# Second half of an attention kernel: half-width weights for Yh, relative outputs in 64 x 64 tiles of the array that fill two banks in turn, eight PSUM banks, eight residual tiles

## The chip, the cores and the metric

The kernel runs on one core of a Trainium2 chip. The metric is the time of one execution on the device in microseconds (us). Its engines are TensorE (PE: matmuls; PEld: their weight loads), VectorE (DVE), ScalarE (ACT), GpSimd (POOL) and SyncE (SP, which issues DMAs here). Matmuls write to PSUM, eight banks of 128 partitions x 512 floats.

## The reference

Eight images, 256 channels, 64 x 64 pixels, 8 heads of 64 channels. `Ix` picks from the table of relative positions.

```python
qkv = einsum('bcxy,oc->boxy', group_norm(x), w_qkv); q, k, v = split(qkv, 3)
k = softmax(k, axis=-1)
context = einsum('ndm,nem->nde', k, v)
content_out = einsum('nde,ndm->nem', context, q)
Px = einsum('xir,rd->xid', Ix, rel_rows);    Sx = einsum('ndxy,xid->nixy', q4, Px)
Yh = einsum('nixy,neiy->nexy', Sx, v4)
Yh = batch_norm(Yh)                          # mean and variance over images, heads and pixels
Py = einsum('yir,rd->yid', Iy, rel_columns); Sy = einsum('ndxy,yid->nixy', q4, Py)
rel_pos_out = einsum('nixy,nexi->nexy', Sy, Yh)
out = einsum('bcxy,oc->boxy', content_out + rel_pos_out, w_out) + b_out
return x + out
```

## The kernel before

The batch norm of Yh needs all images, so the kernel has two halves. The first (to about 1980 us) computes q, the context and Yh and stores them in DRAM. The second, which the change is about, goes over the images again. Every float32 operand is split into a high and a low float16 part, and a product is three matmuls (`TERMS`: high x high, high x low of the second, low of the first x high).

Heads are handled in pairs: `hp` is 0 to 3, head `h` of a pair lies on partitions 64h to 64h+63, and t = 4 x image + hp. The work is cut in tiles that each fill one PSUM bank, of three kinds:

- `sy` (L942), eight a head pair: Sy from q and the table of columns. 32 matmuls of 64 columns; each has 64 weight columns and writes 64 partitions, so a tile uses half the array's columns.
- `ro` (L956 and L962), eight a head pair: the output of 8 of the 64 rows x. The content part (L956) is 8 matmuls of 256 columns. The relative part (L962) is, for each x, three matmuls with 128 x 128 weights from `yb_hi` or `yb_lo` and 64 columns of `sy_hi` or `sy_lo`. These weights are block diagonal: `yb_hi[:, a, h, e, x]` holds head h's Yh on its own 64 partitions, and zeros on the other 64, which POOL writes once (L1141 to L1143).
- `pr` (L976), sixteen an image: the projection, 12 matmuls of 512 columns, for 128 channels and 512 pixels.

`turn2_of` writes the order of the tiles out for the first, a middle and the last image. `sy` tiles of the next head pair stand between the `ro` tiles of this one (`SY_BEFORE`), and the projection of an image between the `ro` tiles of hp 3 and of hp 0 of the next image. All engines go through this order. Tile number n uses bank n mod `BANKS` (5); before it PE waits until DVE has freed that bank (`freed`), so it can be five tiles ahead. ACT takes the high part out of the bank (L1028, L1033), DVE the low part (L1110, L1118), which frees it. For `pr`, ACT adds the bias to a tile of x (`x_res`, four of them, L1023) and DVE adds the bank to it (L1134); this waits for the tile's load from DRAM.

Between the tiles, after each odd `ro`, ACT (L996) and DVE (L1096) split a quarter of the normalised Yh of the next head pair, in two instructions of 64 partitions each, one per head, since the two go to different columns of `yb`. POOL normalises Yh (L1153, L1156). SP loads q for the head pair after next in four chunks, each as soon as a pair of `ro` tiles no longer needs the old one (L851, waits for `filled`), then Yh of the pair after that (L857, 2 MB), the context (L863) and the tiles of x (L869), all in one queue. PE waits for q at the first `sy` tile of a head pair.

Of the kernel before, what the change touches and what calls it, by code (L numbers as in the profile page):

```python
# [29 lines left out]
P = 128  # L30
GN_EPS = 1e-5
BN_EPS = 1e-5
TINY = 1e-30
BANKS = 5
BANK = 512
YST = 2
# [6 lines left out]
def attention_kernel(nc, x, w_qkv_t, w_out_t, b_out, rel_rows_t, rel_cols_t, gamma, beta,  # L43
# [59 lines left out]
    with ExitStack() as top:  # L103
# [8 lines left out]

        bank = ps("bank", [P, BANKS, BANK])
        ctx_ps = ps("ctx_ps", [P, BANK])
        small_ps = ps("small_ps", [P, BANK])
        gn_ps = ps("gn_ps", [P, BANK])

# [627 lines left out]
        SY, RO, PR = 8, 8, CC * 8  # L745
        SY_BEFORE = (0, 0, 0, 0, 1, 3, 5, 8)

        def turn2_of(first=False, final=False):
            order = [("sy", 0, i) for i in range(SY)] if first else []
            for hp in range(HP):  # L750
                done = 0
                for i in range(RO):
                    if hp == 0 and not first and i < RO // 2:
                        order += [("pr", -1, CC * (i + RO // 2) + m) for m in range(CC)]
                    if hp == HP - 1 and not final and i >= RO // 2:
                        order += [("pr", 0, CC * (i - RO // 2) + m) for m in range(CC)]
                    if not (final and hp == HP - 1):
                        order += [("sy", hp + 1, j) for j in range(done, SY_BEFORE[i])]
                        done = SY_BEFORE[i]
                    order.append(("ro", hp, i))  # L760
                    if final and hp == HP - 1 and i >= 2:
                        order += [("pr", 0, CC * (i - 2) + m) for m in range(CC)]
            return order + ([("pr", 0, u) for u in range(PR - 2 * CC, PR)] if final else [])
# [3 lines left out]
        SHIFT2 = len(first_turn2) - NF2  # L767
        assert NF2 % BANKS == 0

# [10 lines left out]
        def evacuated2(b, key):  # L780

            return at2(b, key) + (BANKS + 1)

        def bank_of2(order, n):
            return (n if order is first_turn2 else n + SHIFT2) % BANKS

# [8 lines left out]
        XA = XY // YB  # L795
        XS = 4
        DVE_NORM = (2, 3)

        with ExitStack() as p2, nc.Block() as block:

            q2 = sb("q2", [P, 2, 2, 2, H // XB, HALF, XB], F16, p2)
            y_f = sb("y_f", [P, 2, DK, H], F32, p2)
            yb_hi = sb("yb_hi", [P, H // YB, 2, DK, YB], F16, p2)
            yb_lo = sb("yb_lo", [P, H // YB, 2, DK, YB], F16, p2)
            sy_hi = sb("sy_hi", [P, 2, H, W], F16, p2)
# [39 lines left out]
            def _(sp):  # L845
# [40 lines left out]
                def turn(b, order):  # L886
                    for hp in range(HP):
                        more = order is not final_turn2 or hp + 2 < HP
                        for i in range(RO):
                            if hp == HP - 1 and i in (4, 5) and order is not final_turn2:  # L890
                                for m in range(CC):
                                    load_residual(b, 0, XS + CC * (i - 4) + m)
                            if hp == 0 and i < 2 and order is not first_turn2:
                                for m in range(CC):
                                    load_residual(b, -1, PR - XS + CC * i + m)
                            if i % 2 == 1 and more:
                                c = i // 2
                                sp.wait_ge(filled, at2(b, ("ro", hp, i)) + 1)
                                load_q(b, hp + 2, c)
                            if i == RO - 1 and (order is not final_turn2 or hp + 3 < HP):  # L900
                                sp.wait_ge(yb_lo_done, (b * HP + (hp + 2)) * YC)
                                load_y(b, hp + 3)
                            if i == 1 and more:
                                sp.wait_ge(cb_lo_done, b * HP + (hp + 2))
                                load_context(b, hp + 2)
                            if hp == HP - 2 and i == 5:
                                if order is first_turn2:
                                    sp.wait_ge(stat, 11)
                                    sp.wait_ge(w_split, 3)
                                for u in range(XS):  # L910
                                    load_residual(b, 0, u)
                            if hp == HP - 1 and i == RO - 1 and order is not final_turn2:
                                for u in range(2 * XS, PR - XS):
                                    load_residual(b, 0, u)
# [9 lines left out]
            def _(pe):  # L924
                pe.wait_ge(init, 5)
                pe.wait_ge(stat, 1)
# [3 lines left out]
                def turn(b, order):  # L930
                    for n, (kind, hp, i) in enumerate(order):
                        t = b * HP + hp
                        r = bank_of2(order, n)
                        pe.wait_ge(freed, at2(b, (kind, hp, i)) + 1)
                        if kind == "sy":
                            if i == 0:
# [9 lines left out]
                        elif kind == "ro":  # L946
                            if i == 0:
                                pe.wait_ge(cb_lo_done, t + 1)
                                pe.wait_ge(freed, evacuated2(b, ("sy", hp, SY - 1)))
                            if i % 2 == 0:  # L950
                                pe.wait_ge(yb_lo_done, t * YC + (i // 2 + 1))
                            both = bank[:, r, :].rearrange("p (a x g y) -> p g a x y", x=XB, g=2, y=HALF)
                            for g in range(2):
                                for k, context in enumerate((cb_both, cb_rest)):
                                    for h in range(2):
                                        pe.matmul(both[h * 64:h * 64 + 64, g], context[:, hp % 2, h, :],  # L956
                                                  q2[:, hp % 2, h, g, 4 * i:4 * i + 4, :, :].rearrange("p a y x -> p a x y"),
                                                  start=(g == 0 and k == 0), stop=False, skip_group_check=True)
                            for j in range(8):
                                xx = 8 * i + j  # L960
                                for k, (a, m) in enumerate(TERMS):
                                    mm = pe.matmul(bank[:, r, j * 64:j * 64 + 64],  # L962
                                                   (yb_hi, yb_lo)[a][:, xx // YB, :, :, xx % YB].rearrange("p h e -> p (h e)"),
                                                   (sy_hi, sy_lo)[m][:, hp % 2, xx, :],
                                                   start=False, stop=(j == 7 and k == 2), skip_group_check=True)
                        else:
# [5 lines left out]
                            if hp == -1 and m == 0:  # L972
                                pe.wait_ge(freed, b * NF2 + (SHIFT2 + loop_turn2.index(("ro", HP - 1, nn)) - NF2 + BANKS + 1))
                            for h in range(HP):
# [9 lines left out]
            def _(act):  # L984
# [4 lines left out]
                def split_piece(t, hp, c):  # L989
                    if isinstance(t, int) and t == 0 and c in DVE_NORM:  # L990
                        act.wait_ge(y_norm_b, 2 * (c - DVE_NORM[0]) + 2)
                    else:
                        act.wait_ge(y_norm, t * (2 * YC) + (2 * c + 2))
                    for h in range(2):
                        own = slice(h * 64, h * 64 + 64)
                        o = act.activation(yb_hi[own, c * XA:(c + 1) * XA, h, :, :],  # L996
                                           y_f[own, hp % 2, :, c * XY:(c + 1) * XY].rearrange("p e (a x) -> p a e x", x=YB),
                                           ACT.Copy)
                    o.then_inc(yb_hi_done, 1)

# [47 lines left out]
            def _(dve):  # L1048
                dve.memset(cb_rest[64:128, :, :, :], 0.0).then_inc(init, 1)
                dve.sem_inc(freed, BANKS)  # L1050

# [40 lines left out]
                def split_piece(t, hp, c):  # L1092
                    dve.wait_ge(yb_hi_done, t * YC + (c + 1))
                    for h in range(2):
                        own, s = slice(h * 64, h * 64 + 64), slice(c * XA, (c + 1) * XA)
                        o = dve.tensor_tensor(yb_lo[own, s, h, :, :],  # L1096
                                              y_f[own, hp % 2, :, c * XY:(c + 1) * XY].rearrange("p e (a x) -> p a e x", x=YB),
                                              yb_hi[own, s, h, :, :], ALU.subtract)
                    o.then_inc(yb_lo_done, 1)

# [95 lines left out]
```

## Time and profile before

| | us |
|---|---|
| median of 3 runs | 3277.91 (3276.88 to 3283.99) |
| the profiled execution, its own time | 3290.07 |
| its span | 3288.2 |
| PE, DVE, ACT, POOL busy in the span | 2756.5, 2293.0, 1874.7, 1111.6 |
| mean granted TensorE clock | 0.932 of full speed |

A PE row gives a group of matmuls, or weight loads as PEld. Matmuls overlap in time, so the distance between their starts tells what each costs, and not how long one is busy. "<-issue" is a wait for nothing that the profile shows. A granted clock of 1.00 is 2.4 GHz, 0.50 is 1.2 GHz.

### The profile page before, as it was taken

The page shows a single profiled execution, that of the slowest core. Times are in us where ns is not written, and L with a number is a line of the kernel's source. Part 1 is how long each engine was busy: PE and PEld are TensorE (multiplying, and loading weights), DVE is VectorE, ACT ScalarE, POOL GpSimd, SP SyncE. Part 2 cuts the span into 40 slices and gives each one's busy share as a digit, 9 for nine tenths or more (in the row PEclk, how much of TensorE's full clock was granted, in tenths as well). Part 3 has the DMA queues.
Part 4 walks back from the last instruction along what each step waited for, and adds up shares of the span by engine and source line. Part 5 has one row for each costly group of instructions (what it writes and reads, how often), then busy time and mean ns, then how long its engine had stood idle before and what let it go on. Part 6 is the DMA issues. An engine that isn't in the chain of part 4 may idle for free. (4 is left out here: it accounts for less than half of the span.)

```text
span 3288.2 us, 102882 instructions
## 1 busy us (share of the span) xinstructions
PE 2756.5 (84%) x42610; PEld 2189.8 (67%) x42610; DVE 2293.0 (70%) x3437; ACT 1874.7 (57%) x3268; POOL 1111.6 (34%) x495
## 2 busy tenths in 40 slices
PE   2898998998997988988989981787978787888888
PEld 2687787776876877777778771656565655665655
DVE  5687787786786876787786665756575656665665
ACT  2575665756666666575575652546464545555553
POOL 1223313224133133142241316553434334352530
PEclk9999999999999999999999995898989898989989
DMA  3133323323324224234232336766766757676663
GB/s 131 44 88 112 87 65 118 92 60 118 86 66 131 67 71 139 60 77 127 66 92 56 79 92 130 149 183 145 185 145 172 159 167 171 161 170 160 160 162 105
DMA packets 419610, 381.99 MB, mean 116 GB/s; under 512 B 296784, under 2 KB 363600, under 8 KB 413008
## 3 DMA queue, kind: packets, MB, share of 16 engines
q1 hardware_dynamic: 399632, 341.13, 41.9%
q10 hardware_dynamic: 19520, 34.15, 2.9%
q8 instruction: 361, 5.91, 0.8%
q14 instruction: 97, 0.79, 0.1%
HBM read 206.37 MB, written 168.82 MB: 114 GB/s over the span
## 5 line engine op out<-in xcount | busy, mean ns | idle before, releaser
L365 PE MATMUL bank<-w_hi,x_hi 128*128 128x256 f16 x2048 | 577.9, 282 | 46.6 <-POOL x_lo L700 23.4
L365 PE MATMUL bank<-w_lo,x_hi 128*128 128x256 f16 x2048 | 570.7, 279 | 0.0
L365 PE MATMUL bank<-w_hi,x_lo 128*128 128x256 f16 x2048 | 570.3, 278 | 0.0
L715 POOL TENSOR_TENSOR k_f<-k_f,negmax 128x1024 f32<-128x1024 f32 x64 | 181.6, 2859 | 940.7 <-DVE negmax L675 940.7
L1153 POOL TENSOR_TENSOR y_f<-y_f,y_mul 128x1024 f32<-128x1024 f32 x126 | 264.6, 2100 | 662.9 <-DMA y_f<-y_scratch 661.6
L1096 DVE TENSOR_TENSOR yb_lo<-y_f,yb_hi 64x1024 f16<-64x1024 f32 x256 | 381.7, 1491 | 80.8 <-ACT yb_hi L996 79.1
L652 DVE SCALAR_TENSOR_TENSOR sx_lo<-bank,parity,sx_hi 128x512 f16<-128x512 f32 x512 | 355.2, 743 | 51.7 <-ACT sx_hi L490 51.1
L942 PE MATMUL bank<-q,rc_both 128*64 128x64 f16 x4096 | 282.9, 245 | 97.9 <-issue 47.0
L480 ACT ACTIVATE k_f<-bank 128x256 f32<-128x256 f32 x512 | 198.8, 388 | 244.2 <-PE bank L365 233.8
L490 ACT ACTIVATE sx_hi<-bank,parity 128x512 f16<-128x512 f32 x512 | 321.2, 703 | 26.1 <-PE bank L365 18.4
L942 PEld LDWEIGHTS bank<-q,rc_both 128*64 128x64 f16 x4096 | 252.4, 134 | 125.0 <-issue 76.4
L365 PEld LDWEIGHTS bank<-w_hi,x_hi 128*128 128x128 f16 x2048 | 297.5, 145 | 54.8 <-issue 24.1
L365 PE MATMUL bank<-q_hi,rr_hi 128*128 128x64 f16 x2048 | 241.1, 204 | 100.6 <-DVE ybn L660 58.6
L722 POOL TENSOR_TENSOR p_lo<-k_f,p_hi 128x1024 f16<-128x1024 f32 x128 | 281.1, 2217 | 129.9 <-ACT p_hi L510 129.9
L942 PE MATMUL bank<-q,rc_rest 128*64 128x64 f16 x4096 | 283.9, 245 | 44.0 <-issue 44.0
L365 PEld LDWEIGHTS bank<-w_lo,x_hi 128*128 128x128 f16 x2048 | 301.7, 147 | 3.2
L660 DVE BATCH_NORM_STATS2 ybn<-bank 128x6 f32<-128x512 f32 x256 | 177.9, 695 | 178.8 <-ACT yst L495 178.6
L365 PEld LDWEIGHTS bank<-w_hi,x_lo 128*128 128x128 f16 x2048 | 297.7, 145 | 3.8
L1028 ACT ACTIVATE sy_hi<-bank 128x512 f16<-128x512 f32 x256 | 151.7, 597 | 247.2 <-PE bank L942 245.9
L942 PEld LDWEIGHTS bank<-q,rc_rest 128*64 128x64 f16 x4096 | 258.8, 135 | 43.3 <-issue 43.3
L996 ACT ACTIVATE yb_hi<-y_f 64x1024 f16<-64x1024 f32 x256 | 269.6, 1053 | 26.3 <-DVE y_f L1089 14.7
L616 DVE TENSOR_TENSOR v_lo<-bank,v_hi 128x256 f16<-128x256 f32 x512 | 211.0, 417 | 103.9 <-ACT v_hi L481 103.6
(149 smaller groups left out, 9009.0 us busy)
## 6 DMA issues: line engine op xcount, KB each, us to landing
y_scratch<-yst SPq DMA_DIRECT2D x512, 128.0 KB, 2.0
y_f<-y_scratch SPq DMA_DIRECT2D x64, 1024.0 KB, 11.9
q<-q_scratch SPq DMA_DIRECT2D x256, 256.0 KB, 11.9
x_f<-x SPq DMA_DIRECT2D x16, 2048.0 KB, 10.9
q_scratch<-q_hi SPq DMA_DIRECT2D x64, 512.0 KB, 5.8
q_scratch<-q_lo SPq DMA_DIRECT2D x64, 512.0 KB, 7.4
x_res<-x SPq DMA_DIRECT2D x128, 256.0 KB, 4.3
out<-x_res ACTq DMA_DIRECT2D x128, 256.0 KB, 3.3
```

What stands on the lines that cost most here:

```text
L365: mm = pe.matmul(outs, lhs[a], rhs[m], start=first and n == 0, stop=last and n == 2, **kw)
L480: act.activation(k_f[:, 2 * i:2 * i + 2, :], v[:, :, 0, :], ACT.Copy)
L490: o = act.activation(sx_hi[:, :, g, 8 * i:8 * i + 8], src.rearrange("p (x h) -> p h x", x=8), ACT.Copy, scale=parity[:, g:g + 1])
L616: dve.tensor_tensor(v_lo[:, hp % 2, 2 * i:2 * i + 2, 0:P], v[:, :, 1, :], v_hi[:, hp % 2, 2 * i:2 * i + 2, 0:P], ALU.subtract).then_inc(fr ...
L652: o = dve.scalar_tensor_tensor(sx_lo[:, :, g, s], src.rearrange("p (x h) -> p h x", x=8), parity[:, g:g + 1], sx_hi[:, :, g, s], ALU.mult, ...
L660: dve.bn_stats(ybn[:, hp % HP, i, :], src).then_inc(freed, 1)
L715: pool.tensor_tensor(kk, kk, negmax[:, :].unsqueeze(1).to_broadcast([P, 8, P]), ALU.add).then_inc(shifted_b, 1)
L722: pool.tensor_tensor(p_lo[:, s, :], k_f[:, s, :], p_hi[:, s, :], ALU.subtract).then_inc((p_lo_a, p_lo_b)[j // 2], 1)
L942: mm = pe.matmul(bank[h * 64:h * 64 + 64, r, j * 64:j * 64 + 64], table[:, W - 1 - y:W - 1 - y + 64], q2[:, hp % 2, h, y // HALF, :, y % H ...
L996: o = act.activation(yb_hi[own, c * XA:(c + 1) * XA, h, :, :], y_f[own, hp % 2, :, c * XY:(c + 1) * XY].rearrange("p e (a x) -> p a e x", ...
L1096: o = dve.tensor_tensor(yb_lo[own, s, h, :, :], y_f[own, hp % 2, :, c * XY:(c + 1) * XY].rearrange("p e (a x) -> p a e x", x=YB), yb_hi[ow ...
L1153: pool.tensor_tensor(yy, yy, y_mul[:, :].unsqueeze(2).to_broadcast([P, DK, XY]), ALU.mult).then_inc(y_norm, 1)
```

## The change

The two heads' parts of Yh lose their zeros: `yb_hi` and `yb_lo` are half as big, and a quarter is split in one instruction of 128 partitions. The relative part is computed per head in 64 x 64 tiles of the array, head 0 with the first 64 rows and columns of it and head 1 with the last 64. Two `ro` tiles are filled together: first head 0's part of the one bank and head 1's of the other, then the reverse. The order goes by pairs of `ro` tiles, and `SY_BEFORE` and the places of `pr` go with it. All eight banks take part in the second half (the three that the first half uses for other things among them), and there are eight tiles of x. Of the change without what only renames or counts:

```diff
-        SY_BEFORE = (0, 0, 0, 0, 1, 3, 5, 8)
+        SY_BEFORE = (0, 2, 5, 8)
@@ turn2_of
-                for i in range(RO):
+                for i in range(0, RO, 2):
                     if hp == 0 and not first and i < RO // 2:
-                        order += [("pr", -1, CC * (i + RO // 2) + m) for m in range(CC)]
+                        order += [("pr", -1, CC * (i + RO // 2) + u) for u in range(2 * CC)]
...
                     if not (final and hp == HP - 1):
-                        order += [("sy", hp + 1, j) for j in range(done, SY_BEFORE[i])]
-                        done = SY_BEFORE[i]
-                    order.append(("ro", hp, i))
+                        order += [("sy", hp + 1, j) for j in range(done, SY_BEFORE[i // 2])]
+                        done = SY_BEFORE[i // 2]
+                    order += [("ro", hp, i), ("ro", hp, i + 1)]
...
-        XS = 4
+        XS = 8
-            yb_hi = sb("yb_hi", [P, H // YB, 2, DK, YB], F16, p2)
+            yb_hi = sb("yb_hi", [P, H // YB, DK, YB], F16, p2)
@@ block.sync, turn
-                            if hp == HP - 1 and i in (4, 5) and order is not final_turn2:
-                                for m in range(CC):
-                                    load_residual(b, 0, XS + CC * (i - 4) + m)
...
@@ block.tensor, turn, kind "ro"
-                            if i % 2 == 0:
-                                pe.wait_ge(yb_lo_done, t * YC + (i // 2 + 1))
...
-                            for j in range(8):
-                                xx = 8 * i + j
-                                for k, (a, m) in enumerate(TERMS):
-                                    mm = pe.matmul(bank[:, r, j * 64:j * 64 + 64],
-                                                   (yb_hi, yb_lo)[a][:, xx // YB, :, :, xx % YB].rearrange("p h e -> p (h e)"),
-                                                   (sy_hi, sy_lo)[m][:, hp % 2, xx, :],
-                                                   start=False, stop=(j == 7 and k == 2), skip_group_check=True)
+                            if i % 2 == 1:
+                                continue
+                            pe.wait_ge(yb_lo_done, t * YC + (i // 2 + 1))
+                            pe.wait_ge(freed, at2(b, (kind, hp, i)) + 2)
+                            banks = (r, (r + 1) % BANKS2)
...
+                            def relative(swap):
+                                for j in range(8):
+                                    for k, (a, m) in enumerate(TERMS):
+                                        for h in (swap, 1 - swap):
+                                            own = slice(h * 64, h * 64 + 64)
+                                            xx = 8 * (i + (h ^ swap)) + j
+                                            mm = pe.matmul(bank[own, banks[h ^ swap], j * 64:j * 64 + 64],
+                                                           (yb_hi, yb_lo)[a][own, xx // YB, :, xx % YB],
+                                                           (sy_hi, sy_lo)[m][own, hp % 2, xx, :], start=False,
+                                                           stop=(swap == 1 and j == 7 and k == 2), skip_group_check=True)
+                                            if swap == 1 and j == 7 and k == 2:
+                                                mm.then_inc(filled, 1)
...
+                            content(0, cb_both)
+                            relative(0)
+                            content(1, cb_rest)
+                            relative(1)
@@ block.vector, split_piece (block.scalar's in the same way)
-                    for h in range(2):
-                        own, s = slice(h * 64, h * 64 + 64), slice(c * XA, (c + 1) * XA)
-                        o = dve.tensor_tensor(yb_lo[own, s, h, :, :],
-                                              y_f[own, hp % 2, :, c * XY:(c + 1) * XY].rearrange("p e (a x) -> p a e x", x=YB),
-                                              yb_hi[own, s, h, :, :], ALU.subtract)
-                    o.then_inc(yb_lo_done, 1)
+                    s = slice(c * XA, (c + 1) * XA)
+                    dve.tensor_tensor(yb_lo[:, s, :, :],
+                                      y_f[:, hp % 2, :, c * XY:(c + 1) * XY].rearrange("p e (a x) -> p a e x", x=YB),
+                                      yb_hi[:, s, :, :], ALU.subtract).then_inc(yb_lo_done, 1)
@@ block.gpsimd
-                for tile in (yb_hi, yb_lo):
-                    pool.memset(tile[0:64, :, 1, :, :], 0.0).then_inc(init, 1)
-                    pool.memset(tile[64:128, :, 0, :, :], 0.0).then_inc(init, 1)
```

On PE, a `ro` tile before; this is where the first one of the second half begins (a row with x2 is two matmuls):

```order
7829 L956 MATMUL bank<-q2,cb_both 64x8x32 x2
7830 L956 MATMUL bank<-q2,cb_rest 64x8x32 x2
7831 L956 MATMUL bank<-q2,cb_both 64x8x32 x2
7832 L956 MATMUL bank<-q2,cb_rest 64x8x32 x2
7833 L962 MATMUL bank<-sy_hi,yb_hi 128x64
7834 L962 MATMUL bank<-sy_lo,yb_hi 128x64
7835 L962 MATMUL bank<-sy_hi,yb_lo 128x64
```

And at the same place now, in the middle of the first pair of tiles (L962 is now the content part, L974 the relative part):

```order
7851 L974 MATMUL bank<-sy_hi,yb_hi 64x64 x2
7852 L974 MATMUL bank<-sy_lo,yb_hi 64x64 x2
7853 L974 MATMUL bank<-sy_hi,yb_lo 64x64 x2
7854 L962 MATMUL bank<-q2,cb_rest 64x8x32 x8
7855 L974 MATMUL bank<-sy_hi,yb_hi 64x64 x2
7856 L974 MATMUL bank<-sy_lo,yb_hi 64x64 x2
7857 L974 MATMUL bank<-sy_hi,yb_lo 64x64 x2
```

Each relative matmul of 128 partitions has become two of 64; 24 rows of them stand on each side of row 7854, so a pair of tiles has 96 where two tiles had 48. The content's 16 matmuls a pair are the same ones in another order.

On DVE, the end of the first image (hp 3, with its projection) before:

```order
1053 L1134 SCALAR_TENSOR_TENSOR x_res<-bank,factors,x_res 128x512 x2
1054 L1110 TENSOR_TENSOR sy_lo<-bank,sy_hi 128x64x8
1055 L1118 TENSOR_TENSOR o_lo<-bank,o_hi 128x512
1056 L1134 SCALAR_TENSOR_TENSOR x_res<-bank,factors,x_res 128x512 x2
1057 L1110 TENSOR_TENSOR sy_lo<-bank,sy_hi 128x64x8 x2
1058 L1118 TENSOR_TENSOR o_lo<-bank,o_hi 128x512
1059 L1096 TENSOR_TENSOR yb_lo<-y_f,yb_hi 64x4x256 x2
```

The same stretch now:

```order
1045 L1150 SCALAR_TENSOR_TENSOR x_res<-bank,factors,x_res 128x512 x4
1046 L1126 TENSOR_TENSOR sy_lo<-bank,sy_hi 128x64x8 x3
1047 L1134 TENSOR_TENSOR o_lo<-bank,o_hi 128x512 x2
1048 L1113 TENSOR_TENSOR yb_lo<-y_f,yb_hi 128x1024
1049 L1150 SCALAR_TENSOR_TENSOR x_res<-bank,factors,x_res 128x512 x4
```

The projection comes four tiles at a time, `sy` in twos and threes, and the split of Yh is one instruction in place of two.

On SP, in the first image at hp 2, from the load of the third chunk of q to that of Yh, now:

```order
432 L853 DMA q<-q_scratch 64x4x512 [waits filled2]
433 L853 DMA q<-q_scratch 64x4x512
434 L871 DMA x_res<-x 128x512 [waits out_st0,w_split,stat]
435 L871 DMA x_res<-x 128x512 [waits out_st1]
436 L871 DMA x_res<-x 128x512 [waits out_st2]
437 L871 DMA x_res<-x 128x512 [waits out_st3]
438 L871 DMA x_res<-x 128x512 [waits out_st4]
439 L871 DMA x_res<-x 128x512 [waits out_st5]
440 L871 DMA x_res<-x 128x512 [waits out_st6]
441 L871 DMA x_res<-x 128x512 [waits out_st7]
442 L853 DMA q<-q_scratch 64x4x512 [waits filled2]
443 L853 DMA q<-q_scratch 64x4x512
```

Before, four loads of x stood there and four more between the chunks of hp 3; now eight stand ahead of the last chunk of q of hp 2.

## Rows read from the trace of the kernel before

**Rows 1.** The page: the engines' busy time, and the instruction queue.

```profile
PE 2756.5 (84%) x42610; PEld 2189.8 (67%) x42610; DVE 2293.0 (70%) x3437; ACT 1874.7 (57%) x3268; POOL 1111.6 (34%) x495
...
q8 instruction: 361, 5.91, 0.8%
```

**Rows 2.** Busy time by stretch: six images, one with loads, two inside `sy`.

```profile
core 0: us, PE busy (x) PEld busy (x) DVE busy (x) ACT busy (x) POOL busy (x), PEclk, DMA share, GB/s
2120.00:3080.00 960.00, 791.97 (x13728) 572.45 (x13728) 617.07 (x714) 496.79 (x707) 403.31 (x198) 0.91 0.68 165
2396.00:2416.00 20.00, 13.76 (x347) 12.43 (x344) 15.80 (x21) 11.44 (x17) 6.94 (x4) 0.83 0.95 188
2381.50:2383.40 1.90, 1.90 (x63) 1.90 (x64) 1.90 (x4) 1.81 (x3) 0.00 (x0) 1.00 0.14 36
2411.50:2413.40 1.90, 1.90 (x64) 1.90 (x66) 0.81 (x2) 1.19 (x2) 1.90 (x2) 0.50 1.14 219
```

**Rows 3.** PE's waits, 2120 to 3080 us: us in total, times, longest.

```profile
PE bank L942 <- issue: 81.0, 25, 4.6
PE bank L956 <- DVE x_res L1134: 31.4, 6, 9.8
...
PE bank L942 <- DVE sy_lo L1110: 16.2, 19, 1.1
PE bank L976 <- DVE o_lo L1118: 8.6, 6, 2.0
PE bank L942 <- DVE o_lo L1118: 7.7, 7, 1.2
```

**Rows 4.** PE's waits after 3080 us, in the same columns.

```profile
PE bank L956 <- DVE x_res L1134: 8.8, 1, 8.8
```

**Rows 5.** Timeline of PE at full clock: start, us, instruction.

```profile
2380.59 0.20 PE L962 MATMUL bank<-sy_lo,yb_hi 128*128 128x64 f16 x1
...
2381.32 0.20 PE L962 MATMUL bank<-sy_hi,yb_lo 128*128 128x64 f16 x1
2381.45 0.23 PE L942 MATMUL bank<-q,rc_both 128*64 128x64 f16 x2
...
2383.48 0.31 PE L956 MATMUL bank<-q,cb_both 128*64 128x256 f16 x2
...
2384.06 0.22 PE L962 MATMUL bank<-sy_hi,yb_hi 128*128 128x64 f16 x1
```

**Rows 6.** Timeline of PE at half clock, in a relative part.

```profile
2410.05 0.24 PE L962 MATMUL bank<-sy_lo,yb_hi 128*128 128x64 f16 x1
...
2411.22 0.24 PE L962 MATMUL bank<-sy_hi,yb_lo 128*128 128x64 f16 x1
```

**Rows 7.** Timeline of PE: two stops inside `sy` tiles, and a content part between.

```profile
2408.27 0.26 PE L942 MATMUL bank<-q,rc_both 128*64 128x64 f16 x1 [3.03 <-issue]
...
2408.97 0.45 PE L956 MATMUL bank<-q,cb_both 128*64 128x256 f16 x2
...
2409.99 0.24 PE L962 MATMUL bank<-sy_hi,yb_hi 128*128 128x64 f16 x1
...
2417.51 0.27 PE L942 MATMUL bank<-q,rc_rest 128*64 128x64 f16 x2 [3.71 <-issue]
```

**Rows 8.** Split of Yh on DVE, from the groups after 1970 us: busy us, mean ns.

```profile
L1096 DVE TENSOR_TENSOR yb_lo<-y_f,yb_hi 64x1024 f16<-64x1024 f32 x256 | 381.7, 1491 | 80.8 <-ACT yb_hi L996 79.1
```

**Rows 9.** Timeline of DVE at the start of the second half.

```profile
2001.29 0.22 DVE L1057 TENSOR_SCALAR x_res<-small_ps 128x64 f32<-128x64 f32 x1 [15.82 <-DMA x_res<-w_out_t]
...
2020.65 5.64 DVE L1096 TENSOR_TENSOR yb_lo<-y_f,yb_hi 64x1024 f16<-64x1024 f32 x2 [4.81 <-ACT yb_hi L996]
```

**Rows 10.** DMAs issued from 2344 to 2349 us: KB, median us to landing.

```profile
y_f<-y_scratch SPq DMA_DIRECT2D x2, 1024.0 KB, 10.0
x_res<-x SPq DMA_DIRECT2D x4, 256.0 KB, 13.3
```

**Rows 11.** The same from 2390 to 2391.5 us.

```profile
q<-q_scratch SPq DMA_DIRECT2D x2, 256.0 KB, 3.9
```

More of the change, by code:

```diff
@@ L34 @@
 BANKS = 5
+BANKS2 = 8
 BANK = 512
@@ L111, in sem @@
             return c.enter_context(nc.semaphore(name))
[L113 to L116, printed above, removed]
+        bank = ps("bank", [P, BANKS2, BANK])
+        CTX, SMALL, GN = BANKS, BANKS + 1, BANKS + 2
+        ctx_ps, small_ps, gn_ps = (bank[:, k, :] for k in (CTX, SMALL, GN))
         scale_all = sb("scale_all", [P, 4], F32)
@@ L912, in turn @@
                             if hp == HP - 1 and i == RO - 1 and order is not final_turn2:
-                                for u in range(2 * XS, PR - XS):
+                                for u in range(XS, PR - 4):
                                     load_residual(b, 0, u)
@@ L924, in _ @@
             def _(pe):
[L925 removed]
+                pe.wait_ge(init, 1)
                 pe.wait_ge(stat, 1)
@@ L934, in turn @@
                         pe.wait_ge(freed, at2(b, (kind, hp, i)) + 1)
+                        if order is first_turn2 and r == SMALL and n < BANKS2:
+                            pe.wait_ge(stat, 3)
                         if kind == "sy":
@@ new lines, in turn, with content @@
+                            pe.wait_ge(yb_lo_done, t * YC + (i // 2 + 1))
+                            pe.wait_ge(freed, at2(b, (kind, hp, i)) + 2)
+                            banks = (r, (r + 1) % BANKS2)
+                            def content(k, context):
+                                for j in range(2):
+                                    both = bank[:, banks[j], :].rearrange("p (a x g y) -> p g a x y", x=XB, g=2, y=HALF)
+                                    for g in range(2):
+                                        for h in range(2):
+                                            pe.matmul(both[h * 64:h * 64 + 64, g], context[:, hp % 2, h, :],
+                                                      q2[:, hp % 2, h, g, 4 * (i + j):4 * (i + j) + 4, :, :]
+                                                      .rearrange("p a y x -> p a x y"),
+                                                      start=(g == 0 and k == 0), stop=False, skip_group_check=True)
@@ L993, in split_piece @@
                         act.wait_ge(y_norm, t * (2 * YC) + (2 * c + 2))
-                    for h in range(2):
-                        own = slice(h * 64, h * 64 + 64)
-                        o = act.activation(yb_hi[own, c * XA:(c + 1) * XA, h, :, :],
-                                           y_f[own, hp % 2, :, c * XY:(c + 1) * XY].rearrange("p e (a x) -> p a e x", x=YB),
-                                           ACT.Copy)
-                    o.then_inc(yb_hi_done, 1)
+                    act.activation(yb_hi[:, c * XA:(c + 1) * XA, :, :],
+                                   y_f[:, hp % 2, :, c * XY:(c + 1) * XY].rearrange("p e (a x) -> p a e x", x=YB),
+                                   ACT.Copy).then_inc(yb_hi_done, 1)
                 def store(b, image, u):
@@ L1093, in split_piece @@
                     dve.wait_ge(yb_hi_done, t * YC + (c + 1))
-                    for h in range(2):
-                        own, s = slice(h * 64, h * 64 + 64), slice(c * XA, (c + 1) * XA)
-                        o = dve.tensor_tensor(yb_lo[own, s, h, :, :],
-                                              y_f[own, hp % 2, :, c * XY:(c + 1) * XY].rearrange("p e (a x) -> p a e x", x=YB),
-                                              yb_hi[own, s, h, :, :], ALU.subtract)
-                    o.then_inc(yb_lo_done, 1)
+                    s = slice(c * XA, (c + 1) * XA)
+                    dve.tensor_tensor(yb_lo[:, s, :, :],
+                                      y_f[:, hp % 2, :, c * XY:(c + 1) * XY].rearrange("p e (a x) -> p a e x", x=YB),
+                                      yb_hi[:, s, :, :], ALU.subtract).then_inc(yb_lo_done, 1)
                 split_context(0, 0)
```

25 lines of the change are left out of this document (10 added, 15 removed).

## Prediction

> **What bounds the kernel now.** I read the busy times first, then the stretches of the second half, PE's waits in them, and last PE's timeline matmul by matmul. PE is busy 84% of the span, more than any other engine [rows 1], and 791.97 of the 960 us of the six middle images; DVE is at 617.07, ACT at 496.79, POOL at 403.31 [rows 2]. What PE doesn't use there it mostly loses to four things [rows 3]: 81.0 us in 25 stops inside `sy` tiles that wait for nothing the profile shows, 31.4 us in 6 waits for the residual tile (DVE's L1134 holds the bank, and itself waits for a load of x), and 16.2 + 8.6 + 7.7 = 32.5 us for low parts that DVE hasn't taken out yet. So in the second half the end is set by how fast PE gets through its list, and what counts is the time from start to start.
>
> The timeline gives these distances. In the relative part at full clock 22 starts lie between 2380.59 and 2381.32: 33.2 ns for a matmul of 64 columns with its 128 x 128 weights [rows 5]. At half clock the same 22 take from 2410.05 to 2411.22: 53.2 ns [rows 6], which is 64 columns at 1.2 GHz (53.3 ns); at 2.4 GHz the columns are worth 26.7 ns, and the 33.2 is above it. In `sy`, two tiles from 2381.45 to 2383.48 are 64 matmuls, 31.7 ns each [rows 5]. These already run as two half-arrays side by side, and still two of them cost 63 ns. And the clock makes no difference to them: 1.90 us hold 63 starts at a clock of 1.00 and 64 at 0.50 [rows 2]. A price that halves neither with two tiles in parallel nor doubles with half the clock isn't paid in the array; it belongs to each matmul with its weight load, some 32 ns.
>
> **The change part by part.**
>
> *Relative part on PE.* Before, 8 images x 4 pairs x 8 tiles x 24 = 6144 matmuls. The clock over the six images is 0.91 [rows 2], so 18% of the time is at half: 0.82 x 33.2 + 0.18 x 53.2 = 36.8 ns, 226 us in all. Now there are 12288. The trace has no 64 x 64 tile. Bounds from the rows: if the two tiles of a row overlap entirely and the pair costs what one costs now, 16.6 ns each; if nothing overlaps and the columns count at half clock, 53.2 ns. The row nearest to it is `sy`: also 64 weight columns, 64 moving columns, two tiles in turn. I take its 31.7 ns: 12288 x 31.7 = 390 us. That is +164 us; I keep 160. For a pair of tiles it means 96 x 31.7 = 3.0 us and not 1.6, with twice 0.58 us of content (2383.48 to 2384.06 [rows 5]) beside it: 4.2 us, with the changes of tile shape about 4.4. There are four changes a pair, as before.
>
> The Trainium skill (TensorE: Matmul & The Clock Gate, Back-to-back issue gap) says that a start never follows the one before it by less than about 25 ns, however few columns there are, and that weight load and matmul together set the distance. By its 25 ns the part would take an estimated 307 us, +81 us, and the sum would be 3318. The rows of this case (31.7 and 33.2 ns) lie above that floor and agree with it.
>
> *Stops for nothing visible.* The two shown, 3.03 and 3.71 us, lie inside `sy` tiles in a stretch in which the DMA engines are 95% busy (2396 to 2416) [rows 2, 7], and the program's own instructions come through a DMA queue too (q8, 361 packets with 5.91 MB, 16 KB each [rows 1]). I read the stops as PE running out of instructions. PE has 2304 matmuls with their weight loads an image now and will have 3072, a third more: 81 us in six images, some 106 in eight, grow by a third, +35 us. Above zero and up to +130: after the load of Yh the first `ro` tiles are as dense as `sy` now, also at hp 3, where `pr` thinned them out. I take +45 us.
>
> *Waits that go.* Eight banks and eight tiles of x: PE can do four `pr`, two `ro` and two more `pr` tiles before it needs the first one's bank, 10.4 + 4.4 + 5.2 = 20 us (12 matmuls of 512 columns are 2.6 us at 2.4 GHz), and the load that it waits for lands 13.3 us after its issue, behind that of Yh [rows 10]. So 31.4 + 8.8 = 40 us go [rows 3, 4]. The 32.5 us for low parts go too, for all eight images some 43: three more banks, and DVE works less. Together -83 us; what could be left of it is a third, since the projection still waits for tiles of its own image.
>
> *Splitting Yh.* 256 instructions of 1491 ns on DVE become 128 [rows 8]; if they keep that length (the free size is the same 1024), DVE saves 191 us, ACT in the same way. Neither is on the path but through the waits just counted, so it is 0 there. At the start of the second half it is: PE's first `ro` tile waits for this chain on DVE, three pairs of splits lie in it, and the one shown takes 5.64 us [rows 9]. Half of three such, -8 us.
>
> *Memsets of the zeros.* 0 us: PE's first matmul waited for them, but DVE, which takes its result, starts at 2001.29, when the weights of the projection land [rows 9]. This cover stays.
>
> *Loads.* The first `sy` of a head pair now comes after two `ro` tiles and not after four. The last chunk of q is issued when the tile before is filled and lands 3.9 us later [rows 11]; the pair takes 4.4. At hp 2 eight loads of x (2 MB) stand ahead of it in SP's queue, and SP is behind by their issue. Bounds: 0, and the landing behind a large load, 13.3 us an image [rows 10], +80 over eight with the pair's time off. I take 0.6 us an image, +5.
>
> *Sum.* +160 + 45 - 83 - 8 + 5 = +119 us. The profiled execution took 3290.07 us, so 3409; it is 12.16 us over the median of the runs, and 3277.91 + 119 = 3397. I predict 3395.
>
> **The rivals.**
>
> A. *The two tiles overlap in full.* Head 0's and head 1's matmuls lie on different rows and columns of the array, which `sy`'s do not (they share the rows). If that is what costs 32 ns in `sy`, a pair costs 33.2 ns and each 16.6: 12288 x 16.6 = 204 us, -22. With the waits (-83), the start (-8), loads +5 and +20 for instructions: -88, 3190 us. For it: the rows show no tile that has rows to itself. Against it: the price doesn't move with the clock, so it isn't the array's. The sign turns at (226 + 83 + 8 - 45 - 5) / 12288 = 21.7 ns a matmul; below that the change wins.
>
> The Trainium skill has the rule for A (same page, Packing small matmuls; also TensorEngine Tiling, Theoretical Speedup): tiles on other row and column groups run at the same time, with starts about 4 ns apart. Its measured cases there move 512 columns. By the rule the case would be A or better.
>
> B. *More is lost than I count: the clock.* The granted clock falls after stops (0.83 in the stretch with two of them [rows 2]). If more stops and quarter tiles keep it at half through the `ro` pairs, the content part takes 1.02 us for 0.58 (2408.97 to 2409.99 [rows 7]): 256 x 0.44 = +113 us. And a quarter of the 1536 projection matmuls at half clock (427 for 213 ns by 512 columns) is +82. That is 3590 us. Against it: `sy` without stops, which uses half the array and streams as few columns, runs at a clock of 1.00 [rows 2].
>
> C. *A wash.* Half of the gain of overlap: 22 to 26 ns a matmul would give, from the turning point up, 3278 to 3330. No row speaks for a price between 16.6 and 30.
>
> **How the numbers follow.** My forecast 62%, with its own range from 3320 (28 ns, stops grow by little) to 3480 (stops +130). A 17%. C 9%, of which less than half is inside 0.2% (6.6 us, about what a measurement can tell from no change). B, or loads and stops far above my terms, 12%. Slower by over 0.2%: 62 + 12 + 4 = 78%. Faster: 17 + 1 = 18%. Same: 4%. The range runs from 3220, which leaves out two thirds of A, to 3490, which leaves out most of B.
>
> **What would show it.** In the timeline of the relative part: starts about 31 to 32 ns apart, 96 in 3.0 us (A: pairs at one instant and 33 ns to the next). The wait of L956's successor for `x_res` gone. Waits for `sy_lo` and `o_lo` near zero. Stops "<-issue": more than 25 in six images, now inside relative parts too. Six images take some 90 us more. DVE's split at 128 instructions of about 1.5 us. The forecast is wrong if the distance is under 22 ns, or if the relative part doesn't set the period because waits that I took off stay.

## The result, and the profile after

The changed kernel takes 3374.35 us (median of 4 runs, 3366.86 to 3379.31) against 3280.95 us for the kernel before (4 runs): ratio 1.0265, 95% interval 1.0236 to 1.0295. It is 93 us slower; 114 to 119 us was forecast. Its profiled span is 3373.4 us.

The page of the changed kernel, where rows 1 stood for the kernel before:

```profile
PE 2899.9 (86%) x48754; PEld 2344.6 (70%) x48754; DVE 2098.4 (62%) x3309; ACT 1712.4 (51%) x3140; POOL 1098.0 (33%) x491
...
q8 instruction: 409, 6.70, 0.9%
```

PE has 6144 matmuls more, DVE is busy 195 us less, ACT 162 us less, and the kernel is slower. Where the time went shows in PE's timeline of the changed kernel, at the first content matmul, the first projection of image 0, that of image 6, and the last matmul (start, us, instruction):

```profile
2038.83 0.42 PE L962 MATMUL bank<-q,cb_both 128*64 128x256 f16 x2 [17.25 <-DVE sy_lo L1126]
...
2156.07 0.61 PE L997 MATMUL bank<-o_hi,wo_hi 128*128 128x512 f16 x1
...
3170.07 0.61 PE L997 MATMUL bank<-o_hi,wo_hi 128*128 128x512 f16 x1
...
3369.61 0.38 PE L997 MATMUL bank<-o_hi,wo_lo 128*128 128x512 f16 x1
```

The same four in the kernel before:

```profile
2049.14 0.42 PE L956 MATMUL bank<-q,cb_both 128*64 128x256 f16 x2 [20.85 <-DVE sy_lo L1110]
...
2146.12 0.38 PE L976 MATMUL bank<-o_hi,wo_hi 128*128 128x512 f16 x1 [0.67 <-DVE o_lo L1118]
...
3087.84 0.39 PE L976 MATMUL bank<-o_hi,wo_hi 128*128 128x512 f16 x1 [1.72 <-DVE o_lo L1118]
...
3282.55 0.38 PE L976 MATMUL bank<-o_hi,wo_lo 128*128 128x512 f16 x1
```

The start is 10.3 us earlier; the first image takes 20.3 us more, the six in the middle 72.3 (1014.0 for 941.7, so 169.0 us an image for 157.0), the end 4.8. PE's waits in the changed kernel from 2120 to 3080 us (us in total, times, longest) answer to [rows 3]:

```profile
PE bank L943 <- DMA q<-q_scratch: 36.4, 16, 7.1
PE bank L974 <- issue: 35.7, 12, 5.0
PE bank L943 <- issue: 20.8, 5, 4.8
PE bank L997 <- issue: 12.9, 4, 3.6
PE bank L962 <- issue: 12.9, 7, 2.9
PE bank L997 <- DVE o_lo L1134: 2.9, 1, 2.9
```

The waits for `x_res` and `sy_lo` are gone, as forecast, and 2.9 us are left of those for `o_lo`. The 36.4 us for q are new. The stops for nothing visible are 82 us in 28 stops; before they were 100 us in 31, since two more lines belong to the 81.0 us of [rows 3]:

```profile
PE bank L976 <- issue: 17.8, 5, 3.6
PE bank L956 <- issue: 1.1, 1, 1.1
```

A relative part of the changed kernel in PE's timeline, which answers to [rows 5]:

```profile
2573.38 0.23 PE L974 MATMUL bank<-sy_lo,yb_hi 64*64 64x64 f16 x2
...
2574.70 0.23 PE L974 MATMUL bank<-sy_hi,yb_lo 64*64 64x64 f16 x2
```

From the first of these rows to the second there are 22 steps of two matmuls each in 1.32 us: 60 ns a pair, 30 ns a matmul. The forecast of this price, 31.7 ns, was right within 6%. The granted clock there is 1.00. In this stretch it is 0.50, and 22 steps take 1.32 us again:

```profile
2488.48 0.24 PE L974 MATMUL bank<-sy_lo,yb_hi 64*64 64x64 f16 x2
...
2489.80 0.24 PE L974 MATMUL bank<-sy_hi,yb_lo 64*64 64x64 f16 x2
```

### The profile page after: what moved, and what is told of

Read it like the earlier page. It is cut to its first block and busy times, and to the rows that moved or that the text cites. A ratio compares the mean times of both kernels' runs of the same rounds, so it can differ in the third digit from the quotient of the medians.

```text
span 3373.4 us, 114943 instructions
## 1 busy us (share of the span) xinstructions
PE 2899.9 (86%) x48754; PEld 2344.6 (70%) x48754; DVE 2098.4 (62%) x3309; ACT 1712.4 (51%) x3140; POOL 1098.0 (33%) x491
## 5 line engine op out<-in xcount | busy, mean ns | idle before, releaser
L1134 DVE TENSOR_TENSOR o_lo<-bank,o_hi 128x512 f16<-128x512 f32 x256 | 167.6, 685 | 408.7 <-ACT o_hi L1051 408.7
L974 PE MATMUL bank<-sy_lo,yb_hi 64*64 64x64 f16 x4096 | 382.6, 224 | 25.7 <-issue 25.6
L1051 ACT ACTIVATE o_hi<-bank 128x512 f16<-128x512 f32 x256 | 142.7, 594 | 503.7 <-PE bank L974 502.4
L974 PE MATMUL bank<-sy_hi,yb_lo 64*64 64x64 f16 x4096 | 383.3, 224 | 15.4 <-issue 15.4
L974 PE MATMUL bank<-sy_hi,yb_hi 64*64 64x64 f16 x4096 | 387.3, 227 | 4.3 <-issue 4.2
L943 PE MATMUL bank<-q,rc_both 128*64 128x64 f16 x4096 | 272.6, 244 | 108.2 <-DMA q<-q_scratch 71.5
L974 PEld LDWEIGHTS bank<-sy_hi,yb_hi 64*64 64x64 f16 x4096 | 315.4, 150 | 63.0 <-issue 62.4
L974 PEld LDWEIGHTS bank<-sy_hi,yb_lo 64*64 64x64 f16 x4096 | 321.5, 153 | 42.7 <-issue 42.7
L974 PEld LDWEIGHTS bank<-sy_lo,yb_hi 64*64 64x64 f16 x4096 | 320.8, 153 | 0.0
## 6 DMA issues: line engine op xcount, KB each, us to landing
y_f<-y_scratch SPq DMA_DIRECT2D x64, 1024.0 KB, 12.2
```

Source lines behind the costliest of these rows:

```text
L943: mm = pe.matmul(bank[h * 64:h * 64 + 64, r, j * 64:j * 64 + 64], table[:, W - 1 - y:W - 1 - y + 64], q2[:, hp % 2, h, y // HALF, :, y % H ...
L974: mm = pe.matmul(bank[own, banks[h ^ swap], j * 64:j * 64 + 64], (yb_hi, yb_lo)[a][own, xx // YB, :, xx % YB], (sy_hi, sy_lo)[m][own, hp % ...
L1051: act.activation(o_hi[:, hp, i * BANK:(i + 1) * BANK], src, ACT.Copy).then_inc(hi_done, 1)
L1134: dve.tensor_tensor(o_lo[:, hp, s], src, o_hi[:, hp, s], ALU.subtract).then_inc(freed, 1)
```

## The experiments

In each title stands the ratio to the kernel before, measured on the same chip, with its 95% interval; one hundredth is 33 us. "Window" is the stretch from 2120 to 3080 us.

**e1_full_array: 0.9913 (0.9881 to 0.9945).** The relative part is put back on the whole array. Yh is split in two instructions again, and there are four tiles of x, since eight don't fit. The content part of both tiles now comes first, so a pair of tiles has two changes of tile shape in place of four.

```diff
-                            content(0, cb_both)
-                            relative(0)
-                            content(1, cb_rest)
-                            relative(1)
+                            content(0, cb_both)
+                            content(1, cb_rest)
+                            for j2 in range(2):
...
+                                        mm = pe.matmul(bank[:, banks[j2], j * 64:j * 64 + 64],
+                                                       (yb_hi, yb_lo)[a][:, xx // YB, :, :, xx % YB].rearrange("p h e -> p (h e)"),
...
```

> The changed kernel with the relative part back on the whole array (128 x 128 weights with zeros, 48 matmuls a pair of tiles, Yh split in two instructions); order by pairs and eight banks stay; four residual tiles, since eight don't fit beside the bigger weights. Theory 1, each relative matmul costs some 32 ns whatever part of the array it uses: 12288 x 32.3 ns go and 6144 x 37 ns come, -170 us; the start gives 8 back and the waits for q grow by some 30, as a pair of tiles becomes shorter: 3240 us, under the kernel before. Theory 2, the small tiles run beside each other for free and the slowdown is that of the new order with its waits for q: no gain, 3350 to 3400 us.

115 us faster than the changed kernel (1.0265 - 0.9913) and faster than before. Not all of it is due to the tiles: m5_two_changes below has this order of the content part with the 64 x 64 tiles, and e1_full_array is 93 us faster than that (1.0195 - 0.9913). So the 64 x 64 tiles cost 93 us, less what the halved splitting and the eight tiles of x give; that is as much as the whole change lost. The gain was to be 134 us (3374 to 3240). One wait came back, in the window:

```profile
PE bank L965 <- DVE sy_lo L1126: 59.6, 27, 3.9
```

The first `ro` pair of a head pair needs the last `sy` tile's low part, and with the order by pairs three `sy` tiles stand right before the last pair. PE is faster here and DVE has the doubled splitting again; this run doesn't tell which of the two brings the wait back.

**e4_before_8banks: 0.9854 (0.9810 to 0.9897).** The kernel before with `BANKS2 = 8` in place of 5 for the second half.

> The kernel before with eight banks in the second half, nothing else. Theory 1, the waits for x_res (40 us) and for low parts (some 43 us) go: -70 us, 3210 us. Theory 2, DVE needs 23 us of work in the head pairs without projection and PE 20, so the waits for low parts only move: -40 us, 3240 us.

48 us faster than before. The wait for `x_res` went from 31.4 us to 3.1 in the window. Those for low parts went from 36.2 (the 32.5 of [rows 3] and 3.7 more at L956) to 18.8:

```profile
PE bank L958 <- DVE sy_lo L1112: 10.1, 7, 3.4
PE bank L978 <- DVE o_lo L1120: 7.5, 5, 1.9
...
PE bank L958 <- DVE x_res L1136: 3.1, 1, 3.1
PE bank L944 <- DVE sy_lo L1112: 1.2, 2, 0.6
```

Nearer to theory 2. The banks nearly end the wait for a slow load and halve those for low parts. The stops for nothing visible rose from 100 to 111 us.

**e3_five_banks: 1.0355 (1.0315 to 1.0394).** The changed kernel with `BANKS2 = 5`.

> The changed kernel with five banks in the second half. Theory 1, the three more banks remove the waits for x_res, sy_lo and o_lo, which were 10.5 us an image: +60 to +100 us, 3435 to 3475 us, with the wait for x_res back at the head of each image. Theory 2, a slower PE and a DVE with less to do don't need them: 0 to +15 us.

+30 us, between the two theories: the wait for `x_res` is back (22.4 us, 5 times in the window), those for `sy_lo` are not. So the banks did not end the waits for low parts in the changed kernel. That leaves the halved splitting on DVE, or the slower PE. m6_four_tiles below speaks for the splitting: its relative part is faster, and it waits 1.4 us for low parts.

**e2_sy_later: 1.0190 (1.0144 to 1.0236).** `SY_BEFORE = (0, 0, 4, 8)`.

> The changed kernel with SY_BEFORE (0, 0, 4, 8): the first sy tile of the next head pair stands after four ro tiles, as in the kernel before. Theory 1, PE's waits for q (36.4 us in the six middle images) come from the shorter lead, and are lost time: they go, -45 us, 3330 us. Theory 2, they only stand in for a stop that comes anyway (instructions, load of Yh): less than 10 us.

-25 us, with intervals that just touch (1.0236). The wait for q is gone from the window, all 36.4 us of it, but the stops went from 82 to 101 us:

```profile
PE bank L943 <- issue: 39.2, 10, 5.0
PE bank L974 <- issue: 33.6, 18, 4.4
PE bank L997 <- issue: 27.8, 11, 4.7
```

So some half of the wait for q was lost time of its own, and the rest stood where another stop comes.

**m3_small_loads: 0.9886 (0.9840 to 0.9932).** `load_y` moves 256 of the 4096 elements of a row after the first two loads.

> The changed kernel with a sixteenth of each load of Yh after the first two (the rest of the tile keeps old values). Theory 1, PE's stops for nothing visible are instructions that arrive late behind a DMA burst: both they (82 us in six images' window) and the waits for q (36 us) nearly go, -130 to -160 us, 3220 to 3250 us. Theory 2, the stops come with the number of instructions whatever the DMA engines do: they stay, and only q's waits go, -50 us, 3325 us.

-124 us. The stops inside `sy` and in the content part are gone, those in the relative part are 2.5 us; 13.7 stay at L997, once an image, where the loop's body starts. The waits for q stay too. In m3_small_loads, in the same window:

```profile
PE bank L943 <- DMA q<-q_scratch: 33.6, 19, 4.3
PE bank L997 <- issue: 13.7, 4, 3.5
PE bank L997 <- DVE o_lo L1134: 2.9, 1, 2.9
PE bank L974 <- issue: 2.5, 5, 0.8
```

With the same instructions and 41% of DMA share in place of 61% PE hardly stops. The 66 us that are gone from the window are some 93 in eight images; the granted clock is also higher (0.96 for 0.91 in the window), which may hold the rest of the 124. Theory 1 holds for the stops and failed for q: the waits for q don't come from the load of Yh. The run shows that the load of Yh causes the stops; that they are instructions arriving late is a reading that fits and isn't shown.

Why 30 ns a matmul? My prediction said: a fixed price of each matmul with its load, not of the array. Five runs test that. Four of them show the same stretch of a relative part, from its second row to its last, which is 22 steps; m7_half_weights shows 45 steps. The granted clock is 1.00 in all five stretches.

**m1_32_columns: 1.0285 (1.0221 to 1.0350).** `j * 64:j * 64 + 32` for the output and 32 columns of `sy`.

> The changed kernel with 32 moving columns in each relative matmul in place of 64 (the other 32 output columns get the content part alone). Theory 1, the 32 ns from start to start belong to each matmul with its weight load: starts stay 31 to 32 ns apart, time within 15 us of the changed kernel's. Theory 2, the columns stream at the cost seen: starts some 16 to 20 ns apart, -150 us.

```profile
2567.52 0.21 PE L974 MATMUL bank<-sy_lo,yb_hi 64*64 64x32 f16 x2
...
2568.84 0.21 PE L974 MATMUL bank<-sy_hi,yb_lo 64*64 64x32 f16 x2
```

60 ns a pair, as with 64 columns. The moving columns aren't the price.

**m4_32_weights: 1.0076 (1.0045 to 1.0108).** Weights `0:32` of the 64 columns, output partitions to match.

> The changed kernel with 32 weight columns in each relative matmul in place of 64 (half the output rows get the content part alone). Theory 1, a fixed price for each matmul with its weight load: starts stay 31 to 32 ns apart, within 15 us. Theory 2, the price is the loading of 64 weight columns one after the other for both tiles: starts some 16 to 20 ns apart, -150 us.

```profile
2574.70 0.20 PE L974 MATMUL bank<-sy_lo,yb_hi 64*32 64x64 f16 x2
...
2575.43 0.20 PE L974 MATMUL bank<-sy_hi,yb_lo 64*32 64x64 f16 x2
```

33 ns a pair, 16.6 each, and 62 us off the changed kernel. My theory 1 falls here: with as many matmuls and loads the price nearly halves with the weight columns. The gain isn't 150 us, since in the window the stops rose from 82 to 127 us and the wait for q from 36.4 to 52.1.

**m2_one_head: 1.0096 (1.0057 to 1.0136).** `for h in (0,)`, which leaves out head 1's relative part.

> The changed kernel with the relative part of head 0 alone: 6144 matmuls, all in one 64 x 64 tile, head 1's left out. Theory 1, 32 ns for each: -197 us, 3180 us. Theory 2, the two tiles overlap and a pair costs what one does: no change. Theory 3, without a partner each matmul waits for its own weight load in the same tile, some 50 ns: -70 to -90 us.

```profile
2570.78 0.22 PE L974 MATMUL bank<-sy_lo,yb_hi 64*64 64x64 f16 x1
...
2572.10 0.22 PE L974 MATMUL bank<-sy_hi,yb_lo 64*64 64x64 f16 x1
```

60 ns for a single matmul: the partner was free. The 197 us of theory 1 did not come; 55 us did, and the timeline has them not in the relative part, which takes 48 x 60 ns as before. In the window the waits for nothing visible are 15.2 us at L962 and 12.2 at L974, 27 us for 82: PE uses its instructions at half the rate in the relative part, and stops less.

**m7_half_weights: 1.0046 (1.0033 to 1.0060).** e1_full_array with `0, xx % YB` in place of `:, xx % YB` for the weights: 64 weight columns on 128 rows.

> The kernel of e1_full_array with the left half alone of each 128 x 128 weight in the relative part (64 columns of weights on all 128 rows, output for head 0 alone). Theory 1, 64 columns of weights load in some 60 ns and 128 in less than 33, by another way: starts go up from 33 to some 60 ns though half the weights are left out, +150 us. Theory 2, the time of a load goes with its columns: starts at 27 to 33 ns, the same time or less.

```profile
2568.03 0.23 PE L976 MATMUL bank<-sy_hi,yb_lo 128*64 128x64 f16 x1
...
2570.74 0.22 PE L976 MATMUL bank<-sy_hi,yb_lo 128*64 128x64 f16 x1
```

45 starts in 2.71 us, 60.2 ns, where the 128 x 128 weights took 33.2 [rows 5]. Half the weights left out makes e1_full_array 44 us slower (1.0046 - 0.9913).

**m6_four_tiles: 1.0046 (1.0019 to 1.0074).** For each row x and term, `for h in range(2): for g in range(2)`, with the rows of the array from h and the output partitions from g. Half of the content part stands before the whole relative part of a pair and half behind it, so this kernel too has two changes of tile shape a pair.

> The changed kernel with all four 64 x 64 tiles of the array in turn in the relative part: head h still reads its own rows, but two rows x go side by side, one to output partitions 0 to 63 and one to 64 to 127 (so half of the values land in another place; their number, 12288, is the same). Theory 1, a narrow weight load takes a tile some 60 ns and tiles load beside each other: starts 16 ns apart on average, 12288 x 16 = -195 us in the relative part, of which waits for q and for DVE take back some 50: 3220 to 3240 us. Theory 2, weight loads of one row group go one after the other: still 32 ns on average, no change. Theory 3, two loads in flight is the limit for any reason: no change.

```profile
2507.52 0.23 PE L976 MATMUL bank<-sy_lo,yb_hi 64*64 64x64 f16 x4
...
2508.84 0.24 PE L976 MATMUL bank<-sy_hi,yb_lo 64*64 64x64 f16 x4
```

60 ns for four, 15 ns each: one, two and four tiles take the same time side by side. Yet the kernel gains 72 us and not 140 or more, of which 49 remain against m5_two_changes, which has as few changes of shape. The stops rose from 82 to 155 us, of which two lines are shown, the wait for q from 36.4 to 54.2, and the granted clock is 0.86 for 0.91. That PE uses up its instructions faster than they come is the reading that fits. In the window:

```profile
PE bank L976 <- issue: 104.3, 44, 6.5
PE bank L943 <- DMA q<-q_scratch: 54.2, 16, 6.1
PE bank L943 <- issue: 30.0, 12, 6.3
```

**m5_two_changes: 1.0195 (1.0178 to 1.0212).** In the changed kernel `content(1)` before `relative(0)`: two changes of tile shape a pair and not four.

> The changed kernel with the content part of both tiles first and the relative part after it: two changes of tile shape a pair in place of four. The timelines show some 0.1 us more than the usual distance at each change. Theory 1: 256 changes less by 0.1 us, -25 us against the changed kernel. Theory 2, the array's drain at a change is hidden behind the weight loads: within 8 us.

-23 us against the changed kernel, and the two intervals don't touch: 0.09 us a change. That is theory 1.

**e6_content_ahead: 0.9876 (0.9854 to 0.9898).** e1_full_array with `wait_ge(freed, evacuated2(b, ("sy", hp, SY - 1)))` and the wait for `yb_lo` behind the content matmuls of the pair.

> The kernel of e1_full_array (whole array, eight banks, order by pairs), with PE's waits for the last sy tile and for the low part of Yh behind the content matmuls of the first pair, which need neither. Theory 1, the 59.6 us of waits for sy_lo in six images (27, 2.2 us each) are cut by the 1.1 us that the content of a pair takes, some 30 us in the window and 40 in all: ratio to before 0.98, 3225 us where before is 3290, and under e4_before_8banks. Theory 2, DVE is the bound in the head pairs without projection, and the wait only moves to a later tile: within 10 us of e1_full_array, ratio 0.99.

-12 us against e1_full_array, with intervals that still touch. The wait for low parts fell from 59.6 to 35.4 us, but that for q rose from 8.5 to 29.5. So no gain is shown. Of the kernels with the whole computation e4_before_8banks is the fastest by its median. It beats e1_full_array (all four of its runs, 3230 to 3253 us, lie under all four of that one on the same chip, 3259 to 3263) and isn't told apart from this one (0.9810 to 0.9897 against 0.9854 to 0.9898).

## Why the prediction was right, and where its steps were off

In eight images, with the middle ones as the measure (960 us hold 6.12 images before, 5.68 after):

| step | forecast | measured |
|---|---|---|
| relative part | +160 | 1536 x 30.0 for 768 x 36.8 ns an image: +142 |
| stops for nothing visible | +45 | 14.5 for 16.3 us an image: -15 |
| waits that go | -83 | 0.5 for 11.1 us an image: -85 |
| start | -8 | -10 |
| late q | +5 | 6.4 us an image: +51 |
| sum | +119 | +83 (the two profiled executions: +85; medians: +93) |

The total came out near in part by luck. The stops were forecast 60 us too high and the waits for q 46 us too low, and the two errors cancel for the most part. The step that carries the result, the relative part, was right within 18 us. The prediction's counts of the kernel before were short as well: 81.0 us of stops where the trace has 99.9, and 32.5 us for low parts where it has 36.2.

*Relative part.* The size was right, from `sy` as the nearest row, and the reason given was wrong. I argued that a price which neither doubles at half clock nor falls with two tiles in parallel isn't paid in the array. m1_32_columns, m4_32_weights, m2_one_head and m6_four_tiles show what it goes with. With 64 weight columns the matmuls of one tile follow each other by 60 ns at either clock, whatever the moving columns; with 32 by 33 ns; other tiles do the same at the same time; and with 128 x 128 weights the distance is 33 ns at full clock. That the 60 ns are the weight load's time is the reading that fits; no run has the matmuls without their loads. Rival A was right that the tiles overlap in full and wrong on what one costs. Its sign point of 21.7 ns doesn't hold: m6_four_tiles at 15 ns and m4_32_weights at 16.6 are still slower than the kernel before (1.0046 and 1.0076), since stops and waits for q grew as the relative part got faster. The sum for the sign point held both fixed.

The Trainium skill has this (TensorE: Matmul & The Clock Gate, LDWEIGHTS): a load takes its columns divided by 1.2 ns, whatever the rows, which by estimate is 53 ns for 64 columns and 27 for 32. The runs show 60 and 33 ns from start to start, some 7 ns above both. The Trainium skill also has a fast weight load (same page, Weight-path perf modes) that is only on with the full 128 columns, and the Trainium skill (TensorEngine Tiling, Gotcha 2: Feature Incompatibilities) rules it out with column tiling. m7_half_weights agrees: 60.2 ns for half of the weights that took 33.2; it doesn't tell which of the two conditions counts. This was the rule that spoke against the change, and I weighed the 25 ns floor instead, which doesn't hold across tiles here (16.6 ns in m4_32_weights, 15 in m6_four_tiles).

*Stops.* I scaled them with the number of PE's instructions. That step fails: with a third more of them the stops didn't grow. m3_small_loads shows that the loads of Yh cause the stops, and those are as many as before. They also go with how fast PE uses its instructions. In the relative part a matmul every 60 ns (m2_one_head) came with 27 us of stops in the window, every 30 ns (the changed kernel) with 82, every 16.6 ns (m4_32_weights) with 127 and every 15 ns (m6_four_tiles) with 155; the last three have as many instructions. The pace of 30 ns is near that of the kernel before, 31.7 in `sy` and 33.2 to 53.2 in the relative part.

*Late q.* This step was under-sized ten times. I set a landing of 3.9 us against 4.4 us of a pair and took the margin for real. Of the 36.4 us in the window 27.2 are in six of the 16 waits, one an image: PE's first `sy` tile in hp 3, which needs the last chunk of q that SP asks for in hp 2. In the changed kernel PE stops from 2476 to 2480 us:

```profile
2479.97 0.27 PE L943 MATMUL bank<-q,rc_both 128*64 128x64 f16 x2 [3.77 <-DMA q<-q_scratch]
```

SP's issues of that stretch (start, us, loads; the first of the eight of x lies before it), with the last chunk of q at 2472.13, and the landing of the two loads of q:

```profile
2467.03 4.32 SPq L871 DMA_DIRECT2D x_res<-x  x7
2472.13 1.30 SPq L853 DMA_DIRECT2D q<-q_scratch  x2
...
q<-q_scratch SPq DMA_DIRECT2D x2, 256.0 KB, 6.2
```

SP was not behind, as I had feared: it was done with x at 2471.35, before q could be asked for. But SP needs 0.65 us to issue each of the two loads, they land after 6.2 us (their median) and not 3.9, and the pair lasts 4.2 us. In the other five images the landing at this place is 5.8 to 8.2 us; from 2390 to 2442 us, away from x, it is 4.3. That the 2 MB of x ahead in the queue make the difference is read from this and not tested. The table gives what PE waits; e2_sy_later takes all of it away and gains only 25 us.

*Waits that go, the start, the memsets.* Right. The memsets gave next to nothing, since DVE, which waits for the projection's weights, goes on at 2000.10 us for 2001.29 [rows 9]. That the waits went has two causes: the banks for `x_res`, as e3_five_banks and e4_before_8banks show, and for the low parts less work on DVE, as far as e3_five_banks and m6_four_tiles tell.

*B and C* did not come. The granted clock over the window is 0.91, as before.

## What to carry to other kernels

Zeros in a weight tile can be cheap: matmuls with 128 x 128 weights, half of them zero, followed each other by 33 ns where those with 64 weight columns took 60, so packing heads block-diagonally beat two small tiles in turn. When an experiment puts one part back, look for what else it moves: here the order of the content part came with it, and 23 of 115 us were its own. Before splitting the array, read the distance of starts of a form with the same weight columns that is already in the trace; it carries the price even when its cause isn't understood. Moving a consumer nearer to its load is a cost of its own, to be checked against the issue time and all that is ahead in the queue, and not against the landing alone.

## What the runs showed of the hardware that was not expected

A matmul with 64 weight columns followed the one before in the same tile by 60 ns, with 64 or 32 moving columns, on 64 or 128 rows; with 32 weight columns by 33 ns. Two tiles or four did the same in the same time: 30 and 15 ns a matmul. At 15 ns each PE did not keep going: its stops rose to 155 us of 960, with the DMA engines at 63%. A change between the content part's tile shape and 64 x 64 cost 0.09 us.
